# TensorE sums six combinings with diagonal share blocks, and the refinement of 1/sqrt takes three steps

## The reference, cut to what matters

```
x = x + weights(adj) @ (layernorm(x) @ W + B)      # graph layer, 8192 x 8192
z = layernorm(x)
# mixture of experts: 16 experts, each row goes to its best 2
h = relu(z @ w1[e] + b1[e]);  out_e = h @ w2[e] + b2[e]
y = z + share0 * out_e0 + share1 * out_e1           # the "combining"
x = x + (y - mean(y)) / sqrt(var(y) + 1e-5) * gamma + beta
```

## Time and profile before

| | |
|---|---|
| time, median of 3 runs | 1726.27 us (1724.95 to 1727.42) |
| the profiled execution: its own time, its span | 1723.45 us, 1721.7 us |
| PE, DVE, ACT, POOL busy, share of the span | 92%, 85%, 90%, 29% |
| mean granted TensorE clock | 0.974 |
| L1018, share * result, DVE | x128 |
| L652, normalise, ACT | x64, 26.3 us |

### The profile page before, as it was taken

How to read it: one execution, slowest core, us unless ns; L and a number is a source line. 1 busy time by engine, 2 the same in 40 slices (tenths; PEclk the granted TensorE clock), 3 DMA queues, 4 the chain that set the end, 5 groups by cost and what they waited for, 6 DMA issues and landing times.

```text
span 1721.7 us, 24396 instructions
## 1 busy us (share of the span) xinstructions
PE 1584.9 (92%) x8066; PEld 1041.0 (60%) x8066; DVE 1455.9 (85%) x2105; ACT 1543.5 (90%) x1443; POOL 499.0 (29%) x389
## 2 busy tenths in 40 slices
PE   4999999999999999999999999999999999878740
PEld 3666666666666666666666666556666668877630
DVE  7999989898989898989898999999989982332587
ACT  5899999999999999999999999999999995545553
POOL 0001040404040404040404040804040405777740
PEclk9999999999999999999999999999999999989975
DMA  9558877777676777776767787667777736776864
GB/s 314 157 160 243 234 216 209 208 207 208 206 208 207 208 206 208 207 209 207 209 207 209 207 215 223 201 196 214 208 208 208 208 112 175 208 194 188 259 210 130
DMA packets 239659, 353.49 MB, mean 205 GB/s; under 512 B 20687, under 2 KB 99039, under 8 KB 239408
## 3 DMA queue, kind: packets, MB, share of 16 engines
q1 hardware_dynamic: 230256, 334.93, 67.3%
q0 software_dynamic: 9280, 17.01, 2.8%
HBM read 320.19 MB, written 29.57 MB: 203 GB/s over the span
## 4 chain that ended last, share of the span: by engine, by line
PE 75%; DVE 10%; SPq 5%; issue 3%; DMA 3%; POOL 2%; ACT 1%; DVEq 0%; ACTq 0%; POOLq 0%
PE acc L1132 46%; PE tp L1151 23%; DVE chunk L693 3%; DVE chunk L699 2%; SPq L372 2%; SPq L388 2%; PE tp L1182 2%; DVE chunk L1018 1%; POOL pool_carrier L469 1%; DVE stats L705 1%; DMA chunk<-rows_in 1%; POOL rows_in L496 1%; PE tp L1210 1%; PE acc L1210 1%; PE misc L1108 1%
## 5 line engine op out<-in xcount | busy, mean ns | idle before, releaser
L1132 PE MATMUL acc<-wT,msg 128*128 128x512 f32 x2048 | 973.3, 598 | 0.7 <-DVE yT L799 0.7
L549 ACT ACTIVATE wT<-tp 128x1024 f32<-128x1024 f32 x512 | 726.8, 1584 | 16.1 <-PE tp L1151 16.1
L543 ACT ACTIVATE chunk<-chunk 128x2048 f32<-128x2048 f32 x256 | 633.4, 2474 | 0.1
L699 DVE SCALAR_TENSOR_TENSOR chunk<-chunk 128x2048 f32<-128x2048 f32 x256 | 584.5, 2283 | 57.4 <-ACT chunk L543 57.0
L1151 PEld LDWEIGHTS tp<-ident,chunk 128*128 128x128 f32 x4096 | 478.1, 141 | 223.2 <-issue 220.1
L693 DVE SCALAR_TENSOR_TENSOR chunk<-chunk 128x2048 f32<-128x2048 f32 x256 | 583.2, 2279 | 1.9 <-DMA chunk<-in_adj_dram 1.9
L1151 PE MATMUL tp<-ident,chunk 128*128 128x128 f32 x4096 | 533.5, 273 | 0.0
L1132 PEld LDWEIGHTS acc<-wT,msg 128*128 128x128 f32 x2048 | 348.9, 190 | 256.6 <-issue 245.7
L538 ACT ACTIVATE chunk<-chunk 128x4096 f32<-128x4096 f32 x118 | 499.5, 4233 | 0.0
L469 POOL TENSOR_TENSOR pool_carrier<-pool_carrier 1x1 f32<-1x1 f32 x16 | 50.7, 3168 | 775.2 <-DVE row_now L884 775.1
L496 POOL DMA_INDIRECT rows_in<-y_wide,row_now x128 | 211.9, 1655 | 40.8 <-issue 40.8
(11 more groups left out here) (116 smaller groups left out, 731.0 us busy)
## 6 DMA issues: line engine op xcount, KB each, us to landing
chunk<-in_adj_dram SPq DMA_DIRECT2D x256, 1024.0 KB, 5.4
chunk<-in_L_ffn_w_dram SPq DMA_DIRECT2D x160, 128.0 KB, 2.7
chunk<-rows_in SPq DMA_DIRECT2D x160, 64.5 KB
chunk<-by_token SPq DMA_DIRECT2D x16, 512.0 KB
y_wide<-y_wide SPq DMA_DIRECT2D x16, 256.0 KB, 7.1
y_kept<-y_wide SPq DMA_DIRECT2D x16, 256.0 KB
chunk<-y_kept SPq DMA_DIRECT2D x16, 256.0 KB, 3.9
out_dram<-chunk SPq DMA_DIRECT2D x16, 256.0 KB
```

What stands on the lines that cost most here:

```text
L543: act.activation(slot(c), slot(c), ACT.Exp, scale=-1.0).then_inc(inverted, 1)
L549: act.activation(wT[:, (g * PPG + m) % WSLOTS, :], tp[(g * PPG + m) % TSLOTS][:, :], ACT.Exp, scale=-2.0).then_inc(weighted, 1)
L699: dve.scalar_tensor_tensor(out=slot(c), in0=slot(c), scalar=2.0, in1=slot(c), op0=ALU.subtract, op1=ALU.mult).then_inc(squared, 1)
L1132: ins = pe.matmul(acc[:, :], msg[:, n, :], wT[:, (g * PPG + m) % WSLOTS, k * ROWS:(k + 1) * ROWS], start=(n == 0), stop=(n == 2 * PPG - 1))
```

## The change

`LAST_FIRST` is 10, the first group of the second batch. For groups 10 to 15:

- DVE makes 48 diagonal 128x128 blocks, identity times one column of shares (`make_diag`), one in each of slots 12 to 51 and 64 to 71. 40 lie in spent room of `msg`, 8 in `wT`.
- TensorE sums a group's parts in PSUM (`combine`): for each of 4 tiles two matmuls with a diagonal block as weights and the expert result as moving operand, and one with the identity and z. It waits for the blocks, both loads, and, from group 12 on, for the normalising of group g-2 (its bank is read by then; the two banks are `misc` and half of the first transposing bank).
- DVE's slots 0 and 1 fall away, its statistics wait for TensorE (`z_full`) and read PSUM. ACT normalises from PSUM into the z buffer. `back_free` comes at the statistics, as before.

For all 16 groups the refinement in the combining takes three instructions, (rs^2), ((var+eps)*rs^2), (that - 3)*rs, and gamma is multiplied by -0.5 once in the graph stage. The slots, the starts and COMBINE_PACE stay.

```diff
+        LAST_FIRST = FIRST[-2]
+        DIAGS_AT = RT * 2 * UR + HT * 2 * F
+        IN_MSG = (N // P * D - DIAGS_AT) // P
+        weights_flat = wT[:, :, :].rearrange("p w r -> p (w r)")
+        diags = carve(DIAGS_AT, IN_MSG, P, spent) + carve(0, BATCHES[-1] * KB - IN_MSG, P, weights_flat)
...
+        z_bank = [t.rearrange("p (b d) -> p b d", b=TB) for t in (misc[:, :], first[:, 0:ROWS])]
...
+        DIAG_AT = [12 + j for j in range((BATCHES[-1] - 1) * KB)] + [64 + j for j in range(KB)]
...
                     act.wait_ge(rs_ready, g + 1)
+                    z = z_bank[g % 2] if g >= LAST_FIRST else zs[g % ZS]
                     for b in range(TB):
-                        ins = act.activation(zs[g % ZS][:, b, :], zs[g % ZS][:, b, :], ACT.Identity,
+                        ins = act.activation(zs[g % ZS][:, b, :], z[:, b, :], ACT.Identity,
...
-                if m == 0:
+                if m == 0 and g < LAST_FIRST:
...
-                if m in (0, 1):
+                if m in (0, 1) and g < LAST_FIRST:
...
                 if m == 2:
                     need()
+                    if g >= LAST_FIRST:
+                        dve.wait_ge(z_full, g - LAST_FIRST + 1)
                     dve.sem_inc(back_free, 1)
-                    row_stats(z)
+                    row_stats(z_bank[g % 2] if g >= LAST_FIRST else z)
...
                 if m == 8:
-                    refine(X_PARTS + GROUPS + g, i, rs[:, i, :])
+                    dve.wait_ge(guessed, X_PARTS + GROUPS + g + 1)
+                    need()
+                    link(dve.tensor_tensor(nt[:, :], rs[:, i, :], rs[:, i, :], ALU.mult))
+                    link(dve.scalar_tensor_tensor(out=nt[:, :], in0=mv_now[:, i, :, 1], scalar=EPS, in1=nt[:, :],
+                                                  op0=ALU.add, op1=ALU.mult))
+                    done(dve.scalar_tensor_tensor(out=rs[:, i, :], in0=nt[:, :], scalar=3.0, in1=rs[:, i, :],
+                                                  op0=ALU.subtract, op1=ALU.mult))
...
+            def make_diag(j):
+
+                n, k = divmod(j, KB)
+                if j == 0:
+                    dve.wait_ge(added, WSLOTS + STEPS)
+                dve.tensor_scalar(diags[j], ident[:, :], rows(share, LAST_FIRST + n)[:, k // K, k % K:k % K + 1], None,
+                                  ALU.mult).then_inc(diag_ready, 1)
...
+            def combine(g):
+
+                z, n = z_bank[g % 2], g - LAST_FIRST
+                pe.wait_ge(diag_ready, (n + 1) * KB)
+                pe.wait_ge(z_in[g % ZS], (g // ZS + 1) * 16)
+                pe.wait_ge(back_in[g % BACK], (g // BACK + 1) * 16)
+                if n == 0:
+                    pe.wait_ge(misc_read, 1 + SETUP_MISC * GROUPS + GROUPS * MISC)
+                    pe.wait_ge(rT_ready, NU // 2)
+                if n >= 2:
+                    pe.wait_ge(zn_ready, g - 1)
+                for b in range(TB):
+                    for k in range(K):
+                        pe.matmul(z[:, b, :], diags[n * KB + b * K + k], back[g % BACK][:, b, k, :], start=(k == 0), stop=False)
+                    ins = pe.matmul(z[:, b, :], ident[:, :], zs[g % ZS][:, b, :], start=False, stop=True)
+                ins.then_inc(z_full, 1)
+
+            for g in range(LAST_FIRST, GROUPS):
+                combine(g)
```

More of the change, by code:

```diff
@@ L237, in gnn_moe_kernel @@
         fin_ready = sem("fin_ready")
+        diag_ready = sem("diag_ready")
+        z_full = sem("z_full")
+        gamma_ok = sem("gamma_ok")
         stored = [sem(f"stored{i}") for i in range(FIN)]
@@ L274, in gnn_moe_kernel @@
         LAST = starts[-1] + COMBINE_LONG + 2
+        DIAG_AT = [12 + j for j in range((BATCHES[-1] - 1) * KB)] + [64 + j for j in range(KB)]
+        assert 12 + (BATCHES[-1] - 1) * KB <= 64 and 64 + KB < starts[LAST_FIRST]
         def all_sent(engine, count):
@@ L966, in _ @@
                     done(dve.tensor_copy(nexts[:, :], region0[:, 0, :]))
+                    dve.tensor_scalar(gamma_bc[:, :], gamma_bc[:, :], -0.5, None, ALU.mult).then_inc(gamma_ok, 1)
                 for m in range(PPG):
@@ L1036, in combine_slot @@
                     dve.wait_ge(zn_ready, g + 1)
+                    if g == 0:
+                        dve.wait_ge(gamma_ok, 1)
                     done(dve.tensor_tensor(z, z, gamma_bc[:, :].unsqueeze(1).to_broadcast([P, TB, D]), ALU.mult))
@@ L1055, in _ @@
                 table_slot(len(BATCHES) - 1, i - TABLE_AT)
+                for j in range(BATCHES[-1] * KB):
+                    if i == DIAG_AT[j]:
+                        make_diag(j)
                 for g in range(GROUPS):
```

## The result

| | before | changed |
|---|---|---|
| median of 11 runs | 1726.94 us (1724.61 to 1730.11) | 1732.76 us (1728.77 to 1734.61) |
| profiled execution: time, span | 1723.45, 1721.7 | 1732.50, 1730.7 |

The ratio is 1.0032 with a 95% interval of 1.0023 to 1.0042, so the change costs 5.5 us (4.0 to 7.3). Forecast were +5.0 us and 1731.3. Of all executions compared in this document one is left out, of the kernel before, at 7079 us.

What follows compares the result with a forecast made beforehand. DVE was taken to bound the last stage, then a serial chain through PE's sum. Terms 9.5 - 4.3 - 0.5 + 0.3 = +5.0 us on the median 1726.27 gave 1731.3 us, range 1725 to 1735.5.

Steps and rivals of the forecast that it cites:

- The bound before: Last stage: DVE's work without a hole sets the period, 5.79 us a group; ACT idles waiting for the shift.
- part 1: Second batch: DVE loses the shares' sums and one small step, 2.48 us a group, leaving 3.3 us of own work.
- Part 2, the chain: Shift of g-2 to shift of g-1 runs serially: 3.46 us plus C, period 8.16; four periods cost +9.5 us.
- C: Length of PE's sum of one group, 12 matmuls as 24 records: 4.7 us, bounds 2.85 (full clock) and 5.3 (half).
- The rule on 81 ns a matmul: Skill page's figure for 128-column matmuls: would make C 1.0 us, period 4.5, sum 14.8 us lower; the prediction rejected it.
- Part 3, the head start: Start of last stage: groups 10 and 11 wait for no normalising; shift of 10 at 1684.1, not 1688.43, -4.3 us.
- a stage that starts more than 1 us late: Sign that the prediction is wrong: the last stage starts later than 1675 by more than 1 us.
- Part 4, the end: Behind the shift of 14: path as before, two normalisings at 1.5 us and one small step less, -0.5 us.
- Part 5: Before slot 180: shorter refinement hidden, 0; 48 blocks at 0.22 us each, mostly in DVE's idle time, +0.3 us.
- 1: Rival: PE's bursts run at full clock, C 2.85, period 6.31, 1723.9 us in all; chance 0.15.
- 2: Rival: PE is never waited for; period about 4.7 us, -9.2 us, 1717 in all; chance 0.05.
- Rival 3: Making the blocks slows POOL's sends: +5.3 us in place of 0.3 if half hold one, 1736; chance 0.10.

Runs made afterwards that it cites:

- run with PE kept busy: The change plus ten unread identity matmuls on PE behind each sum of groups 11 to 14; ratio 0.9986 to the kernel before, periods 6.42 to 6.43 us.
- repeated profile of before: The kernel before, unedited, profiled once more; group 10's load issued at 1677.50 against 1670.80, span 1728.4 us, 50.9 us from that load to the end.

## Why the prediction was right, step by step

- **The bound before, and part 1.** Right. Without the sums DVE is busy for 3.1 us a period (forecast 3.3).
- **Part 2, the chain.** Right in each link. Shift to ACT 0.20 (0.19), normalising from PSUM 1.50 (1.5), ACT to PE and PE to DVE 0.14 + 0.13 (0.25), statistics to addition 0.93 (0.91), addition to shift 0.61. Together 3.51 (3.46). The run with PE kept busy tests the formula: 3.51 + 2.92 = 6.43, measured 6.43.
- **C.** 4.31, 5.45, 4.45, 5.47 us, mean 4.92, against 4.7; the bounds 2.85 and 5.3 held but for 0.17. All four bursts began at half clock. In the first and third the clock rose about 3 us into the burst, sooner than the 4.0 that I had read from the earlier trace rows; in the other two it didn't rise before the end. So the mean came out near 4.7 from two bursts shorter than the 4.75 reckoned for such a one, and two longer than 5.3. The sum was +10.5 us for four periods, forecast +9.5.
- **The rule on 81 ns a matmul** (the Trainium skill, TensorE: Matmul & The Clock Gate, Back-to-back issue gap). Twelve matmuls took 2.92 us at the full clock, 243 ns each with the tail. For the float32 operands of this kernel these rows decide, and they are three times the page's figure.
- **Part 3, the head start.** From issue of the load to the shift of 10: 17.63 us before, 13.68 now, -3.95 us (forecast -4.3). In absolute times the shift came at 1687.4, not 1684.1, and my own sign "a stage that starts more than 1 us late" came up; the repeated profile of before shows that this is scatter between executions, which I had only allowed for as an offset of the median. The sum of group 11 had less room than I gave it: PE waited 0.24 us for its load, and DVE began the statistics as soon as it was done.
- **Part 4, the end.** From the shift of 14: 10.11 us before, 9.62 now, -0.49 (forecast -0.5).
- **Part 5.** The blocks took 0.27 to 0.28 us each (median), not 0.22. They cost 0 to 2 us (forecast 0.3). The shorter refinement was costed at 0 ahead of slot 180; the run with it alone is 2.8 us faster in the median, of which 1.5 is tail, so that it may give about 1 us there. That part isn't resolved beyond the intervals.
- **Sum.** 10.5 - 3.95 - 0.5 = +6.1 us of tail, and +5.5 us (4.0 to 7.3) measured in the times. Forecast +5.0. That forecast and measurement differ by only 0.5 us is in part luck: the tail lost 1.4 us more than the terms for it said (6.1 against 4.7), and ahead of the tail the kernel seems to have gained 0.6 where I had added 0.3, an estimate from one profile each.

Of the rivals, 1 and 2 are real states of this kernel: each came about when one thing was changed, at 6.43 and 4.80 us a period. Rival 3, the slowed sends, did not come about. POOL's 160 sends took 158.7 us before and 157.7 after, and 18 of them took over 1.0 us before, 12 after.

## What to carry to other kernels

Moving work from a busy engine to an idle one shortens a period only if the new result isn't waited for by the instruction behind which the next release stands. Write down the loop (who releases whom, once per period) before adding the durations: here the receiving engine's 4.3 to 5.5 us went in whole, and moving the waiting instruction two slots down in its own queue was worth 15 us. For a short burst on TensorE look up the granted clock behind a gap of the same length: here a sum behind 3.2 to 3.5 us of idleness took 4.3 to 5.5 us, and behind 1.3 us 2.92. And count records, not matmuls: a float32 matmul was two.

## What the runs showed of the hardware that was not expected

- Useless work can pay: twenty records of matmul a period, in a gap of 3.5 us, held the clock at 1.00 and took the sum from a mean of 4.92 to 2.92 us.
- Over all kernels of this document, from group 11 on: bursts behind gaps of 0.2 to 2.35 us ran at the full clock throughout; behind 2.91, 3.05 and 3.09 us they began at full and fell to half 0.9 to 1.2 us later; behind 2.99 and behind 3.2 to 3.5 us they began at half.
- The four normalisings of 128x128 took 1.50 us from PSUM and 1.65 from SBUF. Four statistics took 0.89 from PSUM and 0.87 from SBUF.
- Beside the sends it was DVE that had single slow instructions. A block took 268 to 528 ns in `msg` (this view: count, duration ns min/median/max, first and last start, forms), while the sends' median stayed 972:

```profile
L1072 DVE TENSOR_SCALAR msg<-ident,share x40: 268/280/528, 1451.7 to 1498.8; 128x128 f32<-128x128 f32 x40
```

  The Trainium skill (SBUF — State Buffer, SBUF: two separate sides) has a DVE operation in a mode with two ports and a GpSimd operation lock each other out for a whole instruction, whichever starts first. The trace does not show that for these blocks, and no run shows which mode they ran in: 18 of the 48 lay wholly inside a send or scatter of POOL and took 267 to 282 ns, and the 5 beside none took 261 to 281. Of the 11 that took over 300 ns, 9 were under way when a send ended, and 7 of these ended 0.05 us behind its end; the other 2 were under way when a send began. So a hold is seen only at the two ends of a send, it falls on DVE, and not every time: 14 others lay across such an end and took the usual time.
- PE could start on a group's 768 KB 4.1 to 4.7 us after the issue of its results' load (once 5.2), and 6.0 to 6.1 us with the next group's load right behind.
